# A cache scatter by halves of a tile, and weight loads placed behind the rows: one layer on one core

## The reference

```
x = x + attention(x)      # q, k, v projections, RMS norm, rotary positions, 8 heads on 4 key heads,
                          # new k and v are put into a paged cache (blocks of 16 rows, found by a
                          # block table), a window of the last 128 keys, softmax, output projection
x = x + x @ weights1[cond]                 # 32 x 32 matrix for each sample, over tokens
x = x + x @ weights2[subj] + bias[subj]    # the same, with a bias
x = x + lora_ffn(x)       # gate and up 256 -> 1024, silu(gate) * up, down 1024 -> 256, each with a
                          # rank-16 addition chosen by the sample's index
```

## Time and profile before

| What | Value |
|---|---|
| median of 3 timed runs | 253.76 us (253.05 to 255.38) |
| profiled execution, its own time | 252.41 us |
| span of the profiled execution | 250.1 us |
| TensorE busy | 207.7 us (83%), 1995 matmuls |
| VectorE, ScalarE, GpSimd busy | 143.0, 105.2, 70.4 us |
| TensorE's mean granted clock | 0.965 of full speed |
| DMA | 25.25 MB in 64124 packets, 55780 of them under 512 bytes |

### The profile page before, as it was taken

How to read it: one execution, slowest core, us unless ns; L and a number is a source line. 1 busy time by engine, 2 the same in 40 slices (tenths; PEclk the granted TensorE clock), 3 DMA queues, 4 the chain that set the end, 5 groups by cost and what they waited for, 6 DMA issues and landing times.

```text
span 250.1 us, 5105 instructions
## 1 busy us (share of the span) xinstructions
PE 207.7 (83%) x1995; PEld 187.9 (75%) x1995; DVE 143.0 (57%) x494; ACT 105.2 (42%) x291; POOL 70.4 (28%) x82
## 2 busy tenths in 40 slices
PE   2699978475865769959899799999979999899995
PEld 1577867364655658949789789888978988799994
DVE  5749878557656747285636644743664454326522
ACT  2163337656740573158323634632363463213310
POOL 3420047330038750176270443227040022000000
PEclk9999999859779999979999999999999999999999
DMA  6787899927983378899794012002200000010001
GB/s 167 219 173 110 187 190 239 320 73 160 136 222 93 105 182 120 195 202 190 130 156 111 3 42 66 0 3 73 76 1 3 0 3 0 3 42 3 0 3 42
DMA packets 64124, 25.25 MB, mean 101 GB/s; under 512 B 55780, under 2 KB 60836, under 8 KB 63524
## 3 DMA queue, kind: packets, MB, share of 16 engines
q1 hardware_dynamic: 60432, 14.07, 28.4%
q0 software_dynamic: 2944, 10.23, 16.1%
q10 hardware_dynamic: 724, 0.62, 0.8%
HBM read 17.83 MB, written 7.08 MB: 100 GB/s over the span
## 4 chain that ended last, share of the span: by engine, by line
PE 31%; issue 15%; DVE 13%; POOL 10%; DMA 5%; ACT 5%; SPq 4%; POOLq 1%
PE bank L1451 26%; POOL far L662 5%; SPq L542 4%; DMA early<-in_kb,blk_i 4%; POOL prob L676 3%; DVE prob L1084 3%; ACT prob L793 3%; DMA d_raw<-in_Wd 2%; DVE mask L1063 1%; PE bank L1437 1%; POOL near L665 1%; PE bank L1417 1%; POOL prob_near L677 1%; PE bank L1398 1%; DVE gs L1133 1%
## 5 line engine op out<-in xcount | busy, mean ns | idle before, releaser
L662 POOL DMA_INDIRECT far<-table_rows,place_i x32 | 31.5, 983 | 70.8 <-issue 37.2
L793 ACT ACTIVATE prob<-prob,ntop,qscale 128x160 f32<-128x160 f32 x64 | 32.4, 508 | 17.1 <-DVE ntop L1090 17.1
L1451 PE MATMUL bank<-xf_high,gu_high 128*128 128x256 f32 x128 | 39.1, 305 | 0.0
L1451 PE MATMUL bank<-xf_high,gu_low 128*128 128x256 f32 x128 | 36.3, 284 | 0.0
L1451 PE MATMUL bank<-xf_low,gu_high 128*128 128x256 f32 x128 | 36.3, 283 | 0.0
L1133 DVE SCALAR_TENSOR_TENSOR gs<-th,bank 128x256 f32<-128x256 f32 x32 | 13.4, 419 | 27.3 <-ACT th L828 27.0
L676 POOL TENSOR_TENSOR prob<-prob,rden 128x512 f32<-128x512 f32 x12 | 12.7, 1055 | 48.6 <-DVE rden L1109 48.6
L1451 PEld LDWEIGHTS bank<-xf_high,gu_high 128*128 128x128 f32 x128 | 24.6, 192 | 1.4 <-issue 1.0
L1451 PEld LDWEIGHTS bank<-xf_low,gu_high 128*128 128x128 f32 x128 | 24.5, 191 | 0.2
L1451 PEld LDWEIGHTS bank<-xf_high,gu_low 128*128 128x128 f32 x128 | 24.4, 191 | 0.0
L828 ACT ACTIVATE th<-bank 128x256 f32<-128x256 f32 x32 | 12.0, 380 | 24.3 <-PE bank L1451 24.3
(11 more groups left out here) (224 smaller groups left out, 523.2 us busy)
## 6 DMA issues: line engine op xcount, KB each, us to landing
table_rows<-early SPq DMA_DIRECT2D x32, 144.0 KB
table_rows<-far_probs SPq DMA_DIRECT2D x2, 512.0 KB, 3.6
gu_raw<-in_Wg SPq DMA_DIRECT2D x2, 512.0 KB, 5.2
gu_raw<-in_Wu SPq DMA_DIRECT2D x2, 512.0 KB, 5.7
d_raw<-in_Wd SPq DMA_DIRECT2D x2, 512.0 KB, 4.7
out<-xs SPq DMA_DIRECT2D x8, 128.0 KB, 1.9
xs<-in_x ACTq DMA_DIRECT2D x1, 512.0 KB, 5.0
xs<-in_x SPq DMA_DIRECT2D x1, 512.0 KB, 5.7
```

Of the source, the lines that this page charges most:

```text
L662: pool.indirect_dma_start(far[r][:, s, :], None, seen, bass.IndirectOffsetOnAxis(ap=far_i[:, GB * n + s:GB * n + s + 1], axis=0)).then_inc ...
L793: last = act.activation(v, v, ACT.Exp, bias=ntop[r][:, j:j + 1], scale=qscale[:, n, j:j + 1], accum_out=den[r][:, j:j + 1])
L1451: last = pe.matmul(dst, w[a], x[b], start=start and n == 0, stop=stop and n == 2)
```

## The change

**The scatter by groups.** A tile's 72 blocks are now ordered by half: 36 blocks of its first group, then 36 of its second. scatter_rows writes the first half's k and v with 8 DMAs of 36 partitions, then the second half's with 8 more. The two places in the table belong to the halves, no longer to odd and even tiles. The gathers of a pair's first group wait for the first half alone, those of the second for both. The next load of blocks waits for both halves.

**Setup.** VectorE makes eight bits of the length first, then shifts the table, then own_blk, whose semaphore lets TensorE make the slots at once. The length columns, the other four bits and three small matmuls come behind.

**SyncE's queue.** b0 and u0 wait for kv_in of pair 0. Then comes scatter 1, then b1, g1 and u1, then Wd, then scatter 2, then Ad.

**FIRST_ORDER.** up0 stands ahead of ("kt", 0), gate1 ahead of ("scores", 0), and ("den", 0) ahead of up1.

```diff
-BP = BT * SLOTS
+HB = GB * OLD
+BP = 2 * HB
-TILE_ROWS = BK * BLOCK
-TILE_AT = np.array([0, TILE_ROWS + B * T])
+HALF_ROWS = HB * BLOCK
+HALF_AT = np.array([0, HALF_ROWS + NEW_ROWS])
...
-    [("use", "a"), "lora", "adapt", ("mask", 0), ("low", "b1"), ("use", "g0"), "gate0", ("kt", 0), ("use", "u0"),
-     ("use", "b1"), "up0",
-     ("scores", 0), ("mask", 1), "gate1", ("first", 1), "up1", ("den", 0), ("prod", 1), "gate2", "up2",
+    [("use", "a"), "lora", "adapt", ("mask", 0), ("low", "b1"), ("use", "g0"), "gate0", ("use", "u0"),
+     ("use", "b1"), "up0", ("kt", 0), "gate1", ("scores", 0), ("mask", 1), ("first", 1), ("den", 0), "up1", ("prod", 1), "gate2", "up2",
...
-                for raw, come, out_sem, at in ((k_raw, k_in, k_out, 0), (v_raw, v_in, v_out, KH)):
-                    sp.wait_ge(come, 16 * (t + 1))
-                    for g in range(G):
-                        lo = int(TILE_AT[t % 2])
...
+                for half in range(2):
+                    lo = int(HALF_AT[half])
+                    own = slice(half * HB, (half + 1) * HB)
+                    for raw, come, at in ((k_raw, k_in, 0), (v_raw, v_in, KH)):
+                        sp.wait_ge(come, 16 * (t + 1))
+                        for g in range(G):
+                            sp.dma_start(table_rows[lo:lo + HALF_ROWS, at + g * HD:at + (g + 1) * HD].rearrange(
+                                "(p o) d -> p o d", o=BLOCK),
+                                raw[own, g * BLOCK * HD:(g + 1) * BLOCK * HD].rearrange("p (o d) -> p o d", d=HD)
+                            ).then_inc(rows_out[t][half], 16)
+
+            def next_rows(t):
+                for r in R:
+                    sp.wait_ge(kv_in[r], 16 * (GB + 1) * t)
+                scatter_rows(t)
...
+            for r in R:
+                sp.wait_ge(kv_in[r], 16 * (GB + 1))
+            load_b(0)
+            gate_up("u0", Wu, 1, lower)
+            next_rows(1)
+            load_b(1)
             gate_up("g1", Wg, 0, upper)
             gate_up("u1", Wu, 1, upper)
...
-            next_rows(2)
             sp.wait_ge(mixer_psum, 2)
...
+            next_rows(2)
             sp.wait_ge(ssum_ready, SUMS)
...
-                pool.wait_ge(k_out[t], 16 * G)
-                pool.wait_ge(v_out[t], 16 * G)
+                for half in range(r + 1):
+                    pool.wait_ge(rows_out[t][half], 16 * 2 * G)
...
-            for k in range(12):
+            for k in range(11, 3, -1):
```

More of the change, by code:

```diff
@@ L395, in build @@
         v_in = sem("v_in")
-        k_out = [sem(f"k_out{t}") for t in range(NT)]
-        v_out = [sem(f"v_out{t}") for t in range(NT)]
+        rows_out = [[sem(f"rows_out{t}_{half}") for half in range(2)] for t in range(NT)]
         new_out = sem("new_out")
@@ L634, in load_blocks @@
             def load_blocks(t):
-                for dst, src, seen, done in ((k_raw, kb, k_out, k_in), (v_raw, vb, v_out, v_in)):
-                    if t:
-                        pool.wait_ge(seen[t - 1], 16 * G)
+                if t:
+                    for half in range(2):
+                        pool.wait_ge(rows_out[t - 1][half], 16 * 2 * G)
+                for dst, src, done in ((k_raw, kb, k_in), (v_raw, vb, v_in)):
                     pool.indirect_dma_start(dst, None, src.rearrange("n g o d -> n (g o d)"),
-                                            bass.IndirectOffsetOnAxis(ap=blk_i[0:BK, t:t + 1], axis=0)).then_inc(done, 16)
+                                            bass.IndirectOffsetOnAxis(ap=blk_i[:, t:t + 1], axis=0)).then_inc(done, 16)
             pool.wait_ge(blk_ready, 1)
@@ L659, in prepare @@
                     pool.wait_ge(o_psum, n - 1)
[L660 removed]
+                seen = table_rows if r else table_rows[0:HALF_ROWS + NEW_ROWS, :]
                 for s in range(GB):
@@ L1210, in _ @@
             pe.wait_ge(ones_set, 1)
+            pe.wait_ge(slot_ready, 1)
+            pe.matmul(small("slots", BP), own_blk[:, :, :, :].rearrange("s h j b -> s (h j b)"), c3("tile"), start=True,
+                      stop=True).then_inc(slot_psum, 1)
             pe.wait_ge(pos_ready, 1)
+            pe.matmul(small("writer", NW)[:, 0:2], wblk[:, :, :].rearrange("s w n -> s (w n)"), ones[0:B, 0:2],
+                      start=True, stop=True)
             pe.matmul(small("writer", NW)[:, 2:4], c3("spread_writer"), len_f[:, 0:2], start=True, stop=True)
@@ L1214, in _ @@
             pe.matmul(small("lens"), ones[0:B, :], diag_len[:, :], start=True, stop=True)
-            pe.wait_ge(slot_ready, 1)
-            pe.matmul(small("slots", BP), own_blk[:, :, :].rearrange("s j b -> s (j b)"), c3("tile"), start=True, stop=True)
-            pe.matmul(small("writer", NW)[:, 0:2], wblk[:, :, :].rearrange("s w n -> s (w n)"), ones[0:B, 0:2],
-                      start=True, stop=True)
             pe.matmul(wblk_rows, ones[0:B, 0:NW], wblk[:, :, :].rearrange("s w n -> s (w n)"), start=True, stop=True
```

52 lines of the change are left out of this document (23 added, 29 removed).

## The result

The changed kernel takes 261.61 us (median of 4 runs, 260.72 to 262.93), the kernel before beside it 254.57 (253.05 to 258.66): a ratio of 1.030, 95% interval 1.022 to 1.039. It is 3% slower, where 247.7 was predicted. The profiled execution took 260.72 us with a span of 258.3, against 252.41 and 250.1.

A forecast was written before the change was run, and what follows sets the result against it. Transfers were taken to bound the chain up to 110 us, TensorE's FFN matmuls from 131 us. Terms -1.3 - 0.1 - 2.3 - 2.9 + 0.4 = -6.2 us gave 247.7 us, range 245.5 to 249.5.

The forecast's parts named there:

- Setup: VectorE's start: block list some 2 us sooner, but everything behind wblk_rows 0.5 us later (0 to 1).
- b0 and u0 behind pair 0's rows: SyncE's queue: without three loads beside them, pair 0's rows take 4 us, group 1's transposes start sooner: -1.3 us.
- Rival B: Pair 0's rows were held by Wg, A and the mixer blocks, not these loads: 249.4 us, chance 0.10.
- I take 10 and keep 8.6 and 12 as bounds: SyncE's issue of a scatter's sixteen DMAs: 10 us, so b1 is issued at 68.5 and nothing is lost.
- rival A: Scatters are issue bound: a half costs Wo's 0.75 us, a scatter 12.0; 250.6 us, chance 0.15.
- the rule against the split: Trainium skill: disjoint partition halves serialize, below 64 KB mostly overhead; its table gave 15.2 us for sixteen scatter DMAs.
- up0 and den ahead, Wd ahead of scatter 2: Waits before group 2's transposes, its normalising and Wd's split shrink or go: -0.1, -2.3 and -2.9 us.
- Rival D: ScalarE's exponentials are the limit, so den ahead gives 1 us and not 2.3: 248.9 us, chance 0.08.
- Price 0.4 (0 to 1): Ad behind Wd and scatter 2 in SyncE's queue: ScalarE's cast of Ad is held up by 0.4 us.
- landed at 111: Ad's arrival: 8.45 us of issue after scatter 2 ends at 99.3, to 107.7, then landing at 111 us.
- Tile 2's rows are wanted after 131 only.: Scatter 2 behind Wd: its later rows were given no price, as nothing wants them before 131 us.
- Rival C: A half costs as much issue as a whole, 17.2 us per scatter, delaying b1 and Ad: 258.4 us, chance 0.05.

The follow-up runs named there:

- e1: The changed kernel with each tile's rows scattered by eight whole DMAs of 72 partitions again, the rest of the change kept: 254.46 us, ratio 0.999.
- e7: e1 with GpSimd's gathers of group 4 and load of tile 3 moved behind down01: 249.25 us, ratio 0.978.
- e16: The changed kernel with eight whole scatter DMAs, b1 ahead of scatter 1, and GpSimd's gathers of group 4 and load of tile 3 behind down01: 250.34 us.
- e11: The changed kernel with only GpSimd's gathers of group 4 and load of tile 3 moved behind down01: 252.11 us, ratio 0.989.
- e13: The changed kernel with only GpSimd's load of tile 3 moved behind down01, the gathers of group 4 left in place: 254.27 us, ratio 0.998.
- e14: The changed kernel with only GpSimd's gathers of group 4 moved behind down01, the load of tile 3 left in place: 261.43 us, ratio 1.029.
- e4: The kernel before the change with scatter 3 cut into DMAs of different partition counts, to price their issue: 255.52 us, one run.
- e6: The changed kernel with scatter halves of 48 partitions, overlapping in the middle, instead of 36: 261.10 us, ratio 1.023.

## Why the prediction was wrong

- **Setup.** Predicted +0.5. The block list came at 6.11 and not 8.11, as forecast, but scatter 0 began no sooner, at 15.61 (15.48 before). The first far gather came at 35.54 and not at 34 to 34.5. The step that failed: I priced the sixteen issues in scatters 1 and 2 and forgot scatter 0, which took 14.29 us and pushed the new rows from 27.21 to 30.02. It cost little, since the next term covered it.
- **b0 and u0 behind pair 0's rows.** Right: group 1's transposes at 51.15 with no wait (50.5 to 51 forecast), lora 0.88 sooner (1.3 forecast). The last gather of pair 0 was issued at 46.97, so its rows took at most 4.2 us (4 forecast, 7.05 before). b0 was issued at 50.61, so nothing of it stood beside the gathers. Rival B falls.
- **"I take 10 and keep 8.6 and 12 as bounds".** Wrong. A scatter took 13.2 to 14.3. The bounds were made from bytes, from b1's 0.48 and from Wo's 0.75; the last was within 0.05 of the pitch of 0.80, and I weighed it down as "partly held up". That was rival A's price, and A's 12.0 was 1.2 short. b1 was issued at 73.43 and not 68.5: 3.2 of this from the scatter's length, and 1.7 from its start, at 60.19 and not 58.5. It landed at 78.0 and not 73.5, and the stretch lost 3.9 where 0 stood. The estimate of 15.2 for sixteen was 1 to 2 too high, and the rule against the split pointed the right way.
- **up0 and den ahead, Wd ahead of scatter 2.** Right in the mechanism: before up0 TensorE waits 1.45 for b1's low part and not for rows, VectorE's rden is followed by the normalising at 92.10, 3.1 us after the first exponential of group 2 where it was 5.8 (90.73 less 84.91), and d_high waits for nothing. Together 4.55 of the 5.3 forecast, although TensorE ran up0 slowly behind the wait for b1, at a granted clock of 0.52 from 80 to 86 us: a matmul of up0 took 0.41 us and not 0.28, the key transposes of group 2 1.06 and not 0.66. Rival D falls.
- **"Price 0.4 (0 to 1)" for Ad.** The step that failed most: 10.16. Ad's issue was put at 99.3 and began at 108.47, since Wd itself came at 93.17 and not 87.6 (the wait for b1 stands ahead of it) and the scatter took 14.21 and not 10. Even whole, the scatter takes 11.13 to 12.17 in this place (e1, e7, e16), which 8.58 did not tell. The forecast of "landed at 111" then took Ad's issue and landing from before, where no block load ran beside them. In the kernel before, the load of tile 3 follows Ad; five us later it falls into it. e11, e13 and e14 show that this collision, not Ad's place, is the greater part: without it the changed kernel is at 252.1 to 254.3. The wait itself made 8.08 of the 10.16; the clock that TensorE had lost by it made the other 2.08.
- **"Tile 2's rows are wanted after 131 only."** True of TensorE and wrong of GpSimd, which executes in order: the gathers of group 4 stand ahead of the normalising of group 3. In the changed kernel the early half hides this (104.56, normalising at 114.52); in e1 it ate the whole gain, and e7 gave it back.
- **Rival C** had the direction and the first link, b1. By its own formula a scatter of 13.7 would have given -6.2 + 3.7 x 1.5 = -0.65, hence 253.1; "half of the same again at Ad" was its error too. The chance of slower, 0.06, rested almost wholly on it.

The sums meet: -0.88 + 3.91 - 4.55 + 10.16 = +8.64, against a forecast of -6.2. All three signs that were named for being wrong came true: ScalarE waits for b1, it waits for Ad, and scatters take over 12 us.

## What to carry to other kernels

A DMA split in two pays its issue twice (here 13.2 us for sixteen halves against 8.6 for eight whole ones, which held the queue longer than an issue alone costs), and the bill goes to whatever stands behind it in the issuing queue; before splitting, list those and their slack, and price the issue from the nearest small DMA of the same shape, not from bytes. When a transfer moves by some us, look for the block load or gather that used to come after it and now falls beside it, on any queue. And "wanted only later" has to be checked on every in-order engine that waits for it: GpSimd held a multiplication behind gathers that nobody needed yet.

## What the runs showed of the hardware

- The issue of these DMAs costs 0.56 to 0.63 us for 32, 48 or 64 partitions and 0.69 to 0.81 for 8, 9, 18, 24, 36 or 72, whatever their bytes, with one of 23 at 1.01 (e4, one run). Sixteen in a row behind a block load took more with 48 partitions: 12.48 for scatter 1, 0.78 each (e6).
- A block load by indirect DMA beside eight strided loads of 64 KB went with a median of 5.7 us from issue to landing and 10.25 us of issuing; without it they were 3.0 and 6.60 with the gathers still there (e13), and 5.25 of issuing without either (e11).
- The wait for Ad left TensorE idle from 120 to 128 us, and the granted clock was 0.92 from 120 to 124 and 0.50 from 124 to 132, half of that with TensorE busy again. In e1, around a wait of 4.67 us, two stretches of 4 us show 0.59 and 0.56.
